# Attention with the keys on the partitions, in groups of four query tiles, and the row maximum by a product of its own

## The reference

```python
q = split_heads(x @ wq.T) * qk_scale      # 4 heads of 64
k = split_heads(x @ wk.T) * qk_scale
v = split_heads(x @ wv.T)
q, k = (_rope(q), _rope(k))
mask = jnp.where(jnp.tril(jnp.ones((T, T), dtype=bool)), 0.0, -jnp.inf).astype(x.dtype)
energy = jnp.einsum('bhtd,bhld->bhtl', q, k) + mask
attn = jax.nn.softmax(energy, axis=-1)
out = jnp.einsum('bhtl,bhld->bhtd', attn, v)
out = out.transpose(0, 2, 1, 3).reshape(B, T, D)
return out @ wo.T
```

## Time and profile before

| what | value |
|---|---|
| two runs | 2279.22 and 2281.04 us, median 2280.13 us |
| profiled execution, span from first to last instruction | 2278.6 us |
| TensorE busy | 1967.0 us, 86% of the span |
| VectorE busy | 1453.1 us, 64% |
| ScalarE busy | 1361.2 us, 60% |
| GpSimd busy | 805.8 us, 35% |
| mean granted TensorE clock | 0.928 |

### The profile page before, as it was taken

One profiled execution on the slowest core, in us unless ns is written; L12 is line 12 of the kernel. 1 busy time (PEld: TensorE's weight loads), 2 busy tenths in 40 slices (PEclk: granted clock), 3 DMA queues, 4 the chain that ended last, 5 costly groups with the idle time before them and its releaser, 6 DMA issues. The chain is left out here.

```text
span 2278.6 us, 43372 instructions
## 1 busy us (share of the span) xinstructions
PE 1967.0 (86%) x14370; PEld 1800.5 (79%) x14370; DVE 1453.1 (64%) x3388; ACT 1361.2 (60%) x3413; POOL 805.8 (35%) x891
## 2 busy tenths in 40 slices
PE   7899999999999999999999998552177999999990
PEld 6799988888888888888888887451177999999980
DVE  7655676565666666666666676376794566556645
ACT  6666665666666666666566654315175666666655
POOL 2222333323233333233111111100085667666642
PEclk9899999999999999999999999655588999999995
DMA  2000011010001100010000000220004444554428
GB/s 69 21 11 22 22 32 34 22 31 29 27 22 33 32 25 29 23 32 29 20 31 27 24 29 31 78 86 1 0 1 127 148 138 144 162 169 128 149 51 295
DMA packets 91409, 135.85 MB, mean 60 GB/s; under 512 B 16932, under 2 KB 79376, under 8 KB 87148
## 3 DMA queue, kind: packets, MB, share of 16 engines
q1 hardware_dynamic: 75372, 123.52, 15.8%
q0 software_dynamic: 15872, 10.24, 2.7%
HBM read 104.62 MB, written 39.85 MB: 63 GB/s over the span
## 5 line engine op out<-in xcount | busy, mean ns | idle before, releaser
L478 PE MATMUL out_ps<-v_sb,probs_t 128*128 128x64 f32 x4352 | 549.4, 271 | 17.7 <-DVE attn L781 15.2
L478 PEld LDWEIGHTS out_ps<-v_sb,probs_t 128*128 128x128 f32 x4352 | 530.6, 193 | 27.2 <-DVE probs_t L758 20.5
L744 DVE TENSOR_REDUCE part_max<-scores_ps 128x1 f32<-128x512 f32 (+3 forms) x576 | 356.8, 621 | 202.7 <-PE scores_ps L443 148.1
L616 ACT ACTIVATE probs<-scores_ps,neg_max 128x512 f32<-128x512 f32 (+3 forms) x640 | 397.6, 627 | 44.4 <-DVE neg_max L748 42.3
L443 PE MATMUL scores_ps<-k_st,q_parts 128*128 128x512 f32 (+3 forms) x1280 | 410.5, 403 | 11.3 <-ACT probs L616 4.9
L625 ACT COPY probs_t<-probs_t_ps 128x512 f32<-128x512 f32 (+3 forms) x416 | 208.2, 501 | 244.8 <-PE probs_t_ps L460 243.5
L460 PE MATMUL probs_t_ps<-ident,probs 128*128 128x128 f32 x2176 | 347.1, 275 | 1.0 <-DVE probs_t L758 1.0
L460 PEld LDWEIGHTS probs_t_ps<-ident,probs 128*128 128x128 f32 x2176 | 261.4, 142 | 51.2 <-issue 2.4
L1519 PE MATMUL up_ps<-xe_t,w 128*128 128x320 f32 x1920 | 289.2, 310 | 2.2 <-DVE xe_t L1626 1.7
L1519 PEld LDWEIGHTS up_ps<-xe_t,w 128*128 128x128 f32 x1920 | 283.8, 189 | 2.9 <-issue 1.9
L443 PEld LDWEIGHTS scores_ps<-k_st,q_parts 128*128 128x128 f32 x1280 | 200.5, 193 | 25.2 <-ACT probs L616 7.2
(11 more groups left out here) (234 smaller groups left out, 3038.8 us busy)
## 6 DMA issues: line engine op xcount, KB each, us to landing
w_raw<-in_w_expert SPq DMA_DIRECT2D x32, 1536.0 KB
w_raw<-in_w_adapter SPq DMA_DIRECT2D x32, 384.0 KB
x_t<-in_x_t SPq DMA_DIRECT2D x64, 128.0 KB, 2.1
x_row<-in_x SPq DMA_DIRECT2D x64, 128.0 KB, 2.0
x_rows<-x SPq DMA_DIRECT2D x64, 128.0 KB, 1.7
acc_rows<-x SPq DMA_DIRECT2D x64, 128.0 KB, 1.8
ln_x<-acc_rows SPq DMA_DIRECT2D x16, 512.0 KB, 6.3
out_rows_dram<-ln_y SPq DMA_DIRECT2D x16, 512.0 KB, 5.2
```

What stands on the lines that cost most here:

```text
L478: mm = pe.matmul(o_ps[:, h, :], probs_t[:, g % PT_RING, a - lo:a - lo + P], v_sb[:, slot(b, a // P), h, :], start=a == 0, stop=a == t * P)
L616: act.activation(probs[:, g % PROBS_RING, 0:hi - lo], s_ps[:, g % AHEAD, 0:hi - lo], ACT.Exp, bias=neg_max[:, u % 8:u % 8 + 1], accum_out= ...
L744: red = dve.tensor_reduce(neg_max[:, ring:ring + 1] if single else part_max[:, ring, c:c + 1], s_ps[:, g % AHEAD, 0:hi - lo], AX.X, ALU.ma ...
```

## The change

A unit is now a group of four query tiles with one head, and the scores that feed exp stand the other way round: 128 keys on the partitions, 512 queries along the columns (`scores`). Exp then leaves the probabilities as the value product needs them, so their transposes and the copies of these go. The sums come from a column of ones beside v (65 columns), and ScalarE's exp has neither bias nor sums. A negated maximum must now be subtracted per column: it is added by the score product itself, through four more rows. `k2` holds the upper part of k in rows 0 to 63 and ones in rows 64 to 67, `q2` the lower part of q and, in rows 64 to 67, the negated maxima of the four tiles, each in its own 128 columns; that pass has 68 rows (L504).

The maxima come from a product of their own, ahead of time: `row_scores` makes the old scores, queries on the partitions, into the two banks of `rows_ps`. Its first pass multiplies the upper part of q with both parts of k over 128 rows (L474), its second the lower part of q with the upper part of k over 64 rows (L476). VectorE reduces them (`maximum`), TensorE transposes the maxima of a unit (`turn_max`, L487), VectorE places them in `q2` (`place_max`, L760). `attention_plan` spreads these row products over the slots ahead of their unit: of the 640 slots, 427 get one entry, 118 two, 8 three and 87 none, and 17 row products run ahead of slot 0.

The transposed q goes to DRAM in its two parts (`store_q`) and comes back for each unit (`load_q`, three transfers), and `k2` is filled from `k_st` for each four blocks (`load_k2`). `FIRST` is 8, VectorE splits q as well as k (`lower_q`), `out_ps` has two banks, and a group's four tiles are finished one after the other behind it. The order of the batches' tiles, long ones first before, is now plain.

```diff
-ONE = 1
-
-AHEAD = 4
-PROBS_RING = 8
-PT_RING = 4
...
+GROUP = 4
+FIRST = 8
+S_RING = 3
+P_RING = 4
+Q_RING = 6
+K2_RING = 4
+ATTN_RING = 3
+K2_ROWS = HD + GROUP
...
+    groups = [(b, g) for b in range(NB) for g in range(NT // GROUP)]
+    units = [(k, h) for k in range(len(groups)) for h in range(HEADS)]
+    blocks = [GROUP * (groups[k][1] + 1) for k, _ in units]
+    first = [sum(blocks[:u]) for u in range(len(units) + 1)]
+    total = first[-1]
+    chunks = [(u, j) for u, n in enumerate(blocks) for j in range(n)]
...
+    pieces = [[(c, s) for c in range(blocks[u] // GROUP) for s in range(GROUP)] for u in range(len(units))]
+    stream = [[] for _ in range(total + 1)]
+    begins, held, slot = [0] * len(units), [0] * (total + 1), total
+    for u in reversed(range(len(units))):
+        slot = last = min(first[u] - 7, slot)
+        for n, (c, s) in enumerate(reversed(pieces[u])):
+            while slot >= 0 and held[slot] >= (2 if first[u] - slot > 14 else 1):
+                slot -= 1
+            last = slot if n == 0 else last
+            held[max(slot, -1)] += 1
+            stream[max(slot, -1) + 1].insert(0, ("max", u, c, s))
+        stream[max(min(last + 2, first[u] - 5), -1) + 1].append(("turn", u))
+        begins[u] = max(slot, -1)
...
+    finish_at, at = [], 0
+    for i in range(COUNT):
+        apart = 2 if i // GROUP == len(groups) - 1 else 7
+        late = 10 if groups[i // GROUP][1] == 3 and apart > 2 else 1
+        at = max(ends[i // GROUP] + late, at + apart)
+        finish_at.append(at)
...
-        s_ps = ctx.enter_context(nc.psum_tensor("scores_ps", [P, AHEAD, CH], F32))
-        t_ps = ctx.enter_context(nc.psum_tensor("probs_t_ps", [P, 2, CH], F32))
-        o_ps = ctx.enter_context(nc.psum_tensor("out_ps", [P, HEADS, HD], F32))
+        s_ps = ctx.enter_context(nc.psum_tensor("scores_ps", [P, S_RING, CH], F32))
+        r_ps = ctx.enter_context(nc.psum_tensor("rows_ps", [P, 2, CH], F32))
+        o_ps = ctx.enter_context(nc.psum_tensor("out_ps", [P, 2, CH], F32))
...
+        k2 = sb("k2", [P, K2_RING, CH], F32R)
+        q1 = sb("q1", [P, Q_RING, CH], F32R)
+        q2 = sb("q2", [P, Q_RING, CH], F32R)
+        q_st = sb("q_st", [P, 2, 2, HEADS, P], F32R)
...
+            def store_q(n):
+
+                sp.wait_ge(q_lower, n + 1)
+                for part_, to in enumerate(("q_up", "q_low")):
+                    sp.dma_start(dram[to][:, :, n * P:(n + 1) * P].rearrange("h d t -> d h t"),
+                                 raw(q_st[0:HD, n % 2, part_])).then_inc(q_stored[n % 2], 16)
+
+            def load_q(u):
+
+                b, g, h = of_unit(u)
+                r, n = u % Q_RING, b * NT + GROUP * g
+                for last in (n + GROUP - 2, n + GROUP - 1):
+                    sp.wait_ge(q_stored[last % 2], 32 * (last // 2 + 1))
+                if u >= Q_RING:
+                    sp.wait_ge(scores_ready, first[u - Q_RING + 1])
+                tokens = slice(n * P, n * P + CH)
+                for to in (q1[0:HD, r], q1[HD:P, r]):
+                    sp.dma_start(raw(to), dram["q_up"][h, :, tokens]).then_inc(q_loaded[r], 16)
+                sp.dma_start(raw(q2[0:HD, r]), dram["q_low"][h, :, tokens]).then_inc(q_loaded[r], 16)
+
+            def load_k2(q):
+
+                u, c = quads[q]
+                b, g, h = of_unit(u)
+                sp.wait_ge(k_upper, b * NT + GROUP * (c + 1))
+                if q >= K2_RING:
+                    old, oc = quads[q - K2_RING]
+                    sp.wait_ge(scores_ready, first[old] + GROUP * (oc + 1))
+                sp.dma_start(raw(k2[0:HD, q % K2_RING]), raw(k_st[0:HD, h, quad_cols(b, c, CH)]))\
+                  .then_inc(k2_loaded[q % K2_RING], 16)
...
+                reach(pe, rows_seen, e - 1)
+                diagonal = c == g
+                width = (s + 1) * P if diagonal else CH
+                out = r_ps[:, e % 2, 0:width]
+                pe.matmul(out, q1[:, u % Q_RING, s * P:(s + 1) * P], k_st[:, h, quad_cols(b, c, width)],
+                          start=True, stop=False)
+                mm = pe.matmul(out, q2[0:HD, u % Q_RING, s * P:(s + 1) * P], k_st[0:HD, h, quad_cols(b, c, width)],
+                               start=False, stop=not diagonal)
+                if diagonal:
+                    mm = pe.matmul(out[:, width - P:width], ident_b[:], causal[:], start=False, stop=True)
+                mm.then_inc(rows_ready, 1)
...
+            def turn_max(u):
+
+                e = entry_of["turn", u]
+                pe.wait_ge(max_ready, u + 1)
+                reach(pe, rows_seen, e - 1)
+                pe.transpose(r_ps[0:K2_ROWS, e % 2, 0:P], neg_max[:, u % 2, :], ident[:]).then_inc(rows_ready, 1)
...
-                    mm = pe.matmul(out, q_parts[:, m % 2, part_, h, :], k_st[:, h, key_cols(g)],
-                                   start=part_ == 0, stop=part_ == 1 and not diagonal)
...
+                reach(pe, exp_done, g - S_RING + 1)
+                low = lows(g)
+                left = min(low, CH - 2 * P)
+                out = s_ps[:, g % S_RING, left:CH]
+                diagonal = j >= GROUP * grp
+                block_ = slice(j % GROUP * P, (j % GROUP + 1) * P)
+                pe.matmul(out, k_st[:, h, cols(b * NT + j)], q1[:, u % Q_RING, left:CH], start=True, stop=False)
+                mm = pe.matmul(out, k2[0:K2_ROWS, q % K2_RING, block_], q2[0:K2_ROWS, u % Q_RING, left:CH],
+                               start=False, stop=not diagonal)
...
-            def turn(g):
-                lo, hi = keys(g)
-                pe.wait_ge(exp_done, ONE + g + 1)
-
-                if g >= 2:
-                    o = owner[g - 2]
-                    pe.wait_ge(probs_copied[o], ONE + nth[g - 2] + 1)
-                else:
-                    for o in range(2):
-                        pe.wait_ge(probs_copied[o], ONE)
-                for a in range(0, hi - lo, P):
-                    mm = pe.transpose(t_ps[:, g % 2, a:a + P], probs[:, g % PROBS_RING, a:a + P], ident[:])
-                mm.then_inc(probs_turned, 1)
...
-                for a in range(lo, hi, P):
-                    mm = pe.matmul(o_ps[:, h, :], probs_t[:, g % PT_RING, a - lo:a - lo + P],
-                                   v_sb[:, slot(b, a // P), h, :], start=a == 0, stop=a == t * P)
...
+                for s in range(lows(g) // P, GROUP):
+                    mm = pe.matmul(o_ps[:, u % 2, s * (HD + 1):(s + 1) * (HD + 1)], probs[:, g % P_RING, s * P:(s + 1) * P],
+                                   v_sb[:, place(b, j), h, :], start=j == 0 and s == 0, stop=j == GROUP * grp + s,
+                                   skip_group_check=True)
...
             def main(g):
-                if g + AHEAD < CHUNKS:
-                    scores(g + AHEAD)
+                if g + 2 < CHUNKS:
+                    scores(g + 2)
                 if g < CHUNKS:
-                    turn(g)
-                for j in products_at[g] if g < CHUNKS + 2 else ():
-                    multiply(j)
+                    rows_of(stream[g])
+                    multiply(g)
 
             def step(kind, k):
...
-                act.activation(probs[:, g % PROBS_RING, 0:hi - lo], s_ps[:, g % AHEAD, 0:hi - lo], ACT.Exp,
-                               bias=neg_max[:, u % 8:u % 8 + 1], accum_out=sums[:, m % 2, h, c:c + 1])\
-                   .then_inc(exp_done, 1)
...
+                act.activation(probs[:, g % P_RING, low:CH], s_ps[:, g % S_RING, low:CH], ACT.Exp).then_inc(exp_done, 1)
...
+            def lower_q(out_ps, n):
+                dve.wait_ge(q_upper, n + 1)
+                dve.tensor_tensor(q_st[0:HD, n % 2, 1], out_ps[0:HD, :].rearrange("p (h d) -> p h d", h=HEADS),
+                                  raw(q_st[0:HD, n % 2, 0]), ALU.subtract).then_inc(q_lower, 1)
...
+                dve.wait_ge(rows_ready, e + 1)
+                ring = u % 2
+                to = neg_max[:, ring, HD + s:HD + s + 1] if g == 0 else part_max[:, ring, s, c:c + 1]
+                red = dve.tensor_reduce(to, r_ps[:, e % 2, 0:width], AX.X, ALU.max, negate=g == 0)
...
-            def copy(g):
-                lo, hi = keys(g)
-                dve.wait_ge(probs_turned, ONE + g + 1)
-
-                dve.wait_ge(values_done, ONE + max(g - PT_RING + 1, 0))
-                dve.tensor_copy(probs_t[:, g % PT_RING, 0:hi - lo], t_ps[:, g % 2, 0:hi - lo])\
-                   .then_inc(probs_copied[0], 1)
...
+            def place_max(u):
+                e = entry_of["turn", u]
+                dve.wait_ge(rows_ready, e + 1)
+                if u >= Q_RING:
+                    dve.wait_ge(scores_ready, first[u - Q_RING + 1])
+                rows = slice(HD, K2_ROWS)
+                dve.tensor_tensor(q2[rows, u % Q_RING].rearrange("p (a b) -> p a b", a=GROUP),
+                                  r_ps[rows, e % 2, 0:P].unsqueeze(1).to_broadcast([GROUP, GROUP, P]),
```

(49 more changed lines are left out.)

759 lines of the change are left out of this document (347 added, 412 removed).

## The result

The changed kernel takes 2637.53 us (2630.86 to 2644.2 in two executions) against 2280.13: a ratio of 1.156, 95% interval 1.153 to 1.159. The forecast was 2537. The direction and most of the sum held; the time lies some 100 us above the forecast, and one term that the sum left out, the clock, is worth more than that.

The account below looks back on a forecast made before the run. TensorE was taken to bound the attention loop (1299.57 of 1359.8 us busy). Loop +270, prologue -25 and tail +12 made +257 on 2278.6, so 2535.6, forecast 2537 (range 2430 to 2640; the sum's own 2450 to 2620).

Parts of the forecast that it names:

- VectorE late in bursts: Rival, row maxima: 126 slots with two or three row entries each wait 0.69 us, 87 us, giving 2624; chance 0.08.
- The price of the 64-row pass: Row pass on TensorE: each change to 64 rows and back costs 0.34 us (0.24 to 0.39), 640 times, +218.
- The two places of the earlier trace with 6 rows: End of a tile, kernel before: one change of row count there and back priced at 0.27 to 0.39 us.
- the experts' 0.24: Experts' gather, kernel before: 64-row loads among 128-row transposes cost 0.24 us extra, taken as the price's lower end.
- The other terms: TensorE, loop: probs transposes -239, second score product +277, maxima transposes +13, projections +38, value passes +10, early row pairs -12.
- The granted clock: TensorE's clock: left at 0.99 without a price; many short stops lowering it was named as a way to be wrong.
- Idle time: TensorE's waits in the loop, 60.2 us before: -35, with -55 to +50.
- Prologue and tail: Ahead of the loop: it starts near 64 instead of 89.2, -25 (-33 to -17); behind it: +12 (5 to 18).
- Nothing charged for the change of rows: Rival, row pass: 64-row passes hide the next weight load and nothing drains, 218 less, 2319; chance 0.11.
- The 68-row passes pay as well: Rival, score passes with the negated maxima: another 640 x 0.34 us, 2755; chance 0.03.

Follow-up runs that it names:

- the kernel with 128 rows: Changed kernel with the second product of each row entry over 128 rows instead of 64, by a doubled lower part of q; 2339.5 us, 1.026 of the kernel before.
- the kernel before at 64 rows: Kernel before with its second score product over rows 0 to 63 alone; 2448.5 us, 1.073 of the kernel before.
- the narrow product: Changed kernel with the second row product over the first 128 of its columns alone; two executions, 2607.5 and 2675.3 us.

## Why the prediction was right, and where it fell short

The sum was +270 for the loop; it is +363. By the table: work +283 where the terms make +305, idle -43 where I had -35, and the clock 0.44 x (313 - 36) = +122 where I had 0.

That 2637.5 lies inside the stated 2430 to 2640 is luck. The sum's own range ended at 2620; the upper end was moved out for a case that didn't come, VectorE late in bursts, and of the two executions one, 2644.2, lies above it.

- **The price of the 64-row pass, 0.34 (0.24 to 0.39), was right.** The runs show 0.28 where a mask or transpose follows and 0.39 where a value pass does; in all 202 us for my 218. The two places of the earlier trace rows with 6 rows stood for 64 rows well; the experts' 0.24 was the low end, as expected; the reason given, that every load is bare there, wasn't tried by itself.
- **The other terms** hold as a sum: of the 22 us that are missing, 16 are the price's and 6 all the others' (the kernel with 128 rows has 81 us more work than the one before, where these terms make 87). The transposes of probs held TensorE for 245 us in the kernel before, its waits left out, where I counted 239 at 0.11. Fifteen row entries ran ahead of the loop, not 17; the other two of the plan's 17 are transposes of maxima.
- **The granted clock, left at 0.99, is the step that failed.** I named it as a way to be wrong and gave it no price; the loop's clock was 0.91, and 313 us of it at 1.2 GHz cost 122 more than the 36 of the kernel before. Its share of the loop couldn't be read from the kernel before, but its size could: the stretch behind the loop stands at 0.52, so it was a one-sided term that belonged in the sum's bounds, and not a remark.
- **Idle time** fell by 43 (expected 35, with +50 as an end): TensorE takes so long that little else is late. Of the kernels made from the changed one, those with a much shorter loop have 38 to 62 us of it again.
- **Prologue and tail**: the loop starts at 72.2, not 64, at a clock of 0.81 ahead of it where the earlier trace rows has 0.97. The row products ahead of the loop begin at 52.06, as the sum had it (47 and 5), and then take 20.17 us at 1.2 GHz where I had 12:

```profile
52.06:72.23 20.17, 18.43 (x47) 9.56 (x48) 7.99 (x16) 0.00 (x0) 0.00 (x0) 0.50 0.32 90
```

The tail is 34.6 for some 32. Together 11 us over; the stages behind, held untouched, took 813.2 us for 808.6.

The rivals. *Nothing charged for the change of rows* falls with the steps of 0.41 and 0.43, with the 298 us of the 128-row product and with the kernel before at 64 rows. The Trainium skill (TensorE: Matmul & The Clock Gate, LDWEIGHTS (loading the stationary operand)) has a load cost the same whatever its rows. The loads of 0.18 and 0.20 at 511 agree with that, but the 64-row one, and the one behind it, start only with their own pass, and the steps there are the long ones. *The 68-row passes pay as well* falls: 0.23 on both sides, and making them 128 left the work as it was. *VectorE the bound in bursts* falls: 17.6 us of idle time in all.

What the clock hangs on is settled in part. Shown one at a time: without visits at the same passes (128 rows) the half clock goes from 313 to 39 us; with 284 visits fewer to 139; with zeros on 60 idle rows to 133; with a quarter of the columns in the second product to 425. So it isn't a property of the visits alone. How exact these figures are is shown by the two kernels with the lowest clocks, whose two executions stand at 0.854 and 0.831 and at 0.871 and 0.846, with the same passes.

Nor is it set by TensorE's waits alone. They stand where most falls begin: in the loops of all eleven kernels 76 of 81 falls come within 6 us of the start of a stop of 0.4 us or more. But there are 368 such stops, the kernels with 60 us of idle time have 36 to 80 us at half clock, and those with 17 to 20 us have 133 to 425. What the edits change most is how long the clock stays low after a fall in the loop: at most 10.2 us with 128 rows, up to 88.7 in the changed kernel, up to 139.9 with the narrow product. The Trainium skill (TensorE: Matmul & The Clock Gate, HAM oscillation) ties a falling clock to waits between bursts of passes. The trace agrees for seven of the changed kernel's eight falls, behind stops of 0.7 to 1.7 us, and not for the one at 641.6, with TensorE shown busy in 50.00 of 50 us. What stays open is why the kernel before with 64 rows keeps to 74 us with the same 640 visits, and why 7 of the changed kernel's 17 stops are followed by a fall and the others aren't.

## What to carry to other kernels

A pass over 64 rows among passes over 128 isn't half a pass: it cost 0.28 to 0.39 us beside its columns, more than the 0.23 of a whole 128-row pass of 512 columns. So fill the rows (a copy of the operand did it here; zeros were tried on the 68-row pass alone) or put such passes side by side. When a step leaves TensorE less to do in time that is shown as busy, price the granted clock too, from a stretch of the same trace at 1.2 GHz. And ask whether the product is needed: the maximum only shifts the softmax, and without its second product the changed order of work takes 1.0% less than the kernel before, with the 68 rows filled as well 1.5% less.

## What was not expected of the hardware

- Rows filled with zeros are worth time: 68 made 128 took nothing at full clock and brought 71 us, all of it by the clock (0.91 to 0.96 in the loop).
- Taking 82 us of columns away from the 64-row passes brought at most 30 us, as the clock fell from 0.91 to 0.87.
- A 64-row pass between two others of 64 rows stands 0.23 from the next, as a 128-row one does: the row count costs nothing, its change does, about 0.09 ahead and 0.1 behind at each end of a visit.
- The clock mostly falls behind short stops of TensorE (0.7 to 1.7 us for seven of the changed kernel's eight falls), and what makes the loss is how long it then stays low with TensorE shown busy: up to 88.7 us there, at most 10.2 after the falls in the loop with all row products over 128 rows.
